# Small norm operations moved between engines, GpSimd's readout one half-step later, and the second norm two half-steps later

## The chip, the core and the metric

One NeuronCore of a Trainium2 chip runs the whole program. The metric is device time in microseconds (us); of a profiled execution the span from the first to the last instruction is known too. Engines are TensorE (PE; its weight loads are PEld), VectorE (DVE), ScalarE (ACT), GpSimd (POOL) and SyncE (SP), which only issues DMAs. Each runs its own instruction list in order and waits on semaphores for the others. A wait holds up everything behind it on that engine.

## The reference: a Mamba layer, then a mixture of experts

The input is x of shape (32, 512, 256), all in float32. Cut to what matters here:

```python
x = x + attn(layernorm(x))                 # attn(x) itself returns m + skip
x = x + ffn(layernorm(x))

# attn: norm again (with ln_g, ln_b), in_proj to xp and z, causal conv of 4 taps, silu,
# x_proj to dt, B, C; dt = softplus(dt_proj(dt)); then for each of 512 channels and 16 states
h = exp(dt * A) * h + dt * u * B           # a scan over the 512 steps
y = sum over states of h * C  + u * D
# y * silu(z), out_proj, gelu, gated linear unit, + skip

# ffn: shared expert silu(x@g) * (x@u) @ down, times sigmoid(x@gate);
# router softmax, top 8 of 64 experts, capacity 128, gather, expert MLP, weighted scatter
```

Both layer norms have no weights: (x - mean) / sqrt(var + eps). A norm of a row is computed as x * rstd + shift, with shift = -mean * rstd. The skip of the first half needs x plus its norm, which is x * (1 + rstd) + shift; 1 + rstd is called `keep`.

## The kernel before: how the work is laid out

The kernel walks over the 32 sequences. For each there is one *turn* of 32 half-steps (s = 0 to 31): the 512 channels are taken in two halves of 256, and each half has 16 states, so half-step s is one state of one half. In a half-step:

- GpSimd computes the scan's input three half-steps ahead (`scan_input`, line 381) into a ring `hs` of 8 buffers.
- ScalarE computes the decays exp(dt * A) two half-steps ahead (`decays`, line 506), into one of two PSUM pairs; it may only overwrite a pair once the state that stood there has been read.
- VectorE runs the scan (line 1173). For 16 of the half-steps (the table `ON_POOL`) the scan's result goes back into the ring and GpSimd multiplies it by C (`read_state`, line 390); for the others it stays in PSUM and VectorE multiplies it (line 1183).
- TensorE adds the products up over the states (line 810), two half-steps behind (`LAG`).

Between these, every turn does the preparation (`prep_at`) of the next sequence and the end (`post_at`) of the previous one: output projection, gelu, gated unit, the second norm, router, and the shared expert. Tables of half-steps say where each piece stands on each engine. Half-step 21, say, is a place in four lists, not a time. The router's and the shared expert's projections all go through one PSUM bank (`pobank`), so each waits until its predecessor has been read.

The parts that matter for the change, before it:

- Second norm, of the previous sequence: VectorE takes the moments at s = 15 (`moments_x1`, line 1046), ScalarE the reciprocal root at 15 (lines 519, 522), VectorE the shift at 16 (`shift_x1`, line 1066), ScalarE the normed rows at 16 (`norm_x1`, line 544), TensorE transposes them at 17 (line 897), ScalarE reads them at 17 (line 631), TensorE computes the router's logits at 18 (line 904), VectorE reads them at 20 (line 1105), and the shared expert's first projection follows at 19 on TensorE (line 919).
- First norm, of the sequence after the next: moments on VectorE at s = 21, reciprocal roots on ScalarE at 26, and at 30 VectorE computes the shifts (`shifts_x`, line 1060) and `keep` (line 1062). ScalarE uses them a turn later (lines 529, 536).

Turns 2 to 29 run in a hardware loop with two turns to an iteration; the others are written out. Behind the turns comes the part with the routed experts, which the change doesn't touch.

Of the kernel before, what the change touches and what calls it, by code (L numbers as in the profile page):

```python
# [12 lines left out]
P = 128  # L13
# [27 lines left out]
def mamba_moe(nc, x, vectors, in_wT, conv_w, x_wT, dt_wT, a_log, out_wT, glu_wT, router_w, sgu_w, sdown_w, egu_w, edown_w, out, counts, table, ends, bc):  # L41
    ctx = ExitStack()
    with ctx:
# [313 lines left out]
        def _(pool):  # L357
# [50 lines left out]

            def turn(b, h, prep, post):
                p = b + 1  # L410
                for s in range(NS):
                    if s == SIZES[1]:
                        step_sizes(b, 1)
                    if s == INPUTS[1]:
                        step_inputs(b, h, 1)
                    if prep and s == SIZES[0]:
                        step_sizes(p, 0)
                    if prep and s == INPUTS[0]:
                        step_inputs(p, 1 - h, 0)
                    to = ahead(b, h, s, LEAD, prep)  # L420
                    if to:
                        scan_input(*to)
                    if s in ON_POOL:
                        read_state(b, h, s)

            step_sizes(0, 0)
            step_inputs(0, 0, 0)
            for n in range(LEAD):
                scan_input(0, 0, 0, n)
            turns(pool, turn)  # L430

# [54 lines left out]
        def _(act):  # L486
# [22 lines left out]
            def scales_x(k):  # L509
                act.wait_ge(ln0, 3 * k + 2)  # L510
                act.activation(rstd[:, 0, :].unsqueeze(2), mv[:, 0, :, 1:2], ACT.Ln, bias=EPS)
                act.activation(rstd[:, 1, :].unsqueeze(2), mv[:, 0, :, 1:2], ACT.Ln, bias=EPS * EPS,
                               scale=1.0 + EPS).then_inc(scales0_ready, 1)
                act.wait_ge(scales0_ready, 4 * k + 1)
                act.activation(rstd[:, 0:2, :], rstd[:, 0:2, :], ACT.Exp, scale=-0.5).then_inc(scales0_ready, 1)

            def scales_x1(k):
                act.wait_ge(ln2, 3 * k + 2)
                act.activation(rstd[:, 2, :].unsqueeze(2), mv[:, 1, :, 1:2], ACT.Ln, bias=EPS)\
                    .then_inc(scales2_ready, 1)  # L520
                act.wait_ge(scales2_ready, 3 * k + 1)
                act.activation(rstd[:, 2, :], rstd[:, 2, :], ACT.Exp, scale=-0.5).then_inc(scales2_ready, 1)

            def norm_x(p):
                act.wait_ge(scales0_ready, 4 * p + 4)
# [14 lines left out]
            def norm_x1(q):  # L540
                act.wait_ge(scales2_ready, 3 * q + 3)
# [496 lines left out]
        def _(dve):  # L1038
# [14 lines left out]
            def moments_x(p):  # L1053
                dve.wait_ge(x_loaded, 16 * p + 16)
                wait(dve, scales0_ready, 4 * p)
                moments(ln0, 0, p, xin)

            def shifts_x(k):
                dve.wait_ge(scales0_ready, 4 * k + 2)
                dve.scalar_tensor_tensor(shift[:, 0:2, :], mv[:, 0, :, 0].unsqueeze(1).broadcast_to([P, 2, NT]), -1.0,  # L1060
                                         rstd[:, 0:2, :], ALU.mult, ALU.mult).then_inc(scales0_ready, 1)
                dve.tensor_scalar(keep[:, :], rstd[:, 0, :], 1.0, None, ALU.add).then_inc(scales0_ready, 1)

            def shift_x1(k):
# [73 lines left out]
            def post_at(q, h, s):  # L1138
# [8 lines left out]
                if s == SHIFT2:  # L1147
                    shift_x1(q)
# [16 lines left out]
            def turn(b, h, prep, post):  # L1165
                for s in range(NS):
# [33 lines left out]
            shifts_x(1)  # L1200
# [83 lines left out]

LAG = 2
# [18 lines left out]
SHIFT2 = 16  # L1304
# [8 lines left out]
NORM2 = 16  # L1313
# [15 lines left out]
XT_AT = (17, 17)  # L1329
R_AT = 18  # L1330
# [54 lines left out]
```

## Time and profile before

| what | value |
|---|---|
| median of 3 runs | 4608.77 us (4603.74 to 4612.37) |
| the profiled execution's own time | 4609.06 us |
| its span | 4607.3 us |
| VectorE busy | 3889.2 us (84%) |
| GpSimd busy | 4003.9 us (87%) |
| TensorE busy | 3685.3 us (80%) |
| ScalarE busy | 3164.8 us (69%) |
| granted TensorE clock, mean | 0.870 |

The turns fill the time from about 80 us to about 4170 us, the routed experts the last 350 us. Busy shares are means over both. The span and the execution's own time differ by 1.8 us, and that time is 0.3 us from the median. In the rows further on a line number such as L1066 is the line of the kernel before.

### The profile page before, as it was taken

How to read it: one execution, taken by the hardware profiler on the slowest of the kernel's cores; microseconds unless marked ns; L12 is line 12 of the kernel's file. 1: busy time of each engine (PE TensorE's matmuls, PEld its weight loads, DVE VectorE, ACT ScalarE, POOL GpSimd, SP SyncE). 2: the span in 40 equal slices, each digit the busy share in tenths (PEclk: the TensorE clock that was granted, in tenths of full speed). 3: DMA queues.
4: the chain of work that ended last, by engine and by line, in shares of the span. 5: the costliest groups of instructions: out<-in, count | busy, mean ns of one | idle time of the engine just before them, and what ended most of it. 6: DMA issues, size and time to landing. Idle time of an engine off the chain costs nothing.

```text
span 4607.3 us, 55489 instructions
## 1 busy us (share of the span) xinstructions
PE 3685.3 (80%) x16000; PEld 2374.8 (52%) x16000; DVE 3889.2 (84%) x4054; ACT 3164.8 (69%) x4931; POOL 4003.9 (87%) x1934
## 2 busy tenths in 40 slices
PE   4688888888888888888888888888888888877455
PEld 2455555555555555555555555555555555553344
DVE  4899889998989989998999899998999899993433
ACT  4677777777777777777877777777777777763111
POOL 3999889998999989998989999899999898991576
PEclk7789888899889989898989988898988898888666
DMA  3222222222222222222222212222222222210665
GB/s 121 88 99 81 70 97 83 73 99 100 95 99 97 68 86 91 66 95 99 99 95 99 90 61 99 83 70 99 99 98 97 100 66 84 91 57 17 174 158 131
DMA packets 147381, 423.29 MB, mean 92 GB/s; under 512 B 15521, under 2 KB 98657, under 8 KB 113777
## 3 DMA queue, kind: packets, MB, share of 16 engines
q1 hardware_dynamic: 123504, 362.73, 21.3%
q0 software_dynamic: 23552, 56.64, 6.5%
q8 instruction: 154, 2.52, 0.2%
q14 instruction: 171, 1.39, 0.1%
HBM read 333.17 MB, written 52.59 MB: 84 GB/s over the span
## 4 chain that ended last, share of the span: by engine, by line
DVE 27%; issue 23%; PE 19%; POOL 18%; ACT 9%; DMA 2%; DVEq 1%; POOLq 0%; ACTq 0%; SPq 0%
POOL hs L381 11%; DVE ps L1173 10%; DVE hs L1173 6%; POOL hs L390 4%; PE ps L871 4%; ACT ps L506 3%; PE ps L810 3%; PE ps L834 3%; PE ps L880 2%; PE ps L854 2%; DVE xc L1075 2%; PE ps L799 2%; ACT L488 1%; DVE stats L1046 1%; PE ps L904 1%
## 5 line engine op out<-in xcount | busy, mean ns | idle before, releaser
L381 POOL TENSOR_TENSOR hs<-dtu,b_all 128x1024 f32<-128x1024 f32 x1024 | 2426.8, 2422 | 0.8
L506 ACT ACTIVATE ps<-dt,neg_a 128x512 f32<-128x512 f32 x2048 | 1326.3, 683 | 506.4 <-DVE hs L1183 288.9
L390 POOL TENSOR_TENSOR hs<-hs,c_all 128x1024 f32<-128x1024 f32 x512 | 1228.4, 2399 | 311.5 <-DVE hs L1173 311.2
L1173 DVE TENSOR_TENSOR_SCAN hs<-ps,hs 128x1024 f32<-128x1024 f32 x512 | 1167.5, 2281 | 190.4 <-ACT ps L506 153.5
L810 PEld LDWEIGHTS ps<-ident,hs 128*128 128x128 f32 x8192 | 1042.8, 153 | 503.0 <-issue 421.7
L810 PE MATMUL ps<-ident,hs 128*128 128x128 f32 x8192 | 1170.7, 294 | 88.2 <-issue 46.7
L1173 DVE TENSOR_TENSOR_SCAN ps<-ps,hs 128x1024 f32<-128x1024 f32 x512 | 1169.5, 2284 | 64.4 <-ACT ps L506 61.6
L1183 DVE TENSOR_TENSOR hs<-ps,c_all 128x1024 f32<-128x1024 f32 x512 | 626.2, 1223 | 28.9
L919 PE MATMUL ps<-mT,w_sgu 128*128 128x512 f32 x1024 | 508.5, 620 | 86.7 <-ACT hid L660 43.1
L834 PE MATMUL ps<-xnT,w_in 128*128 128x512 f32 x512 | 273.1, 660 | 88.4 <-DVE xc L1075 86.1
L1075 DVE SCALAR_TENSOR_TENSOR xc<-ps,cw_sb,xc 128x509 f32<-128x509 f32 (+2 forms) x384 | 285.5, 743 | 34.3 <-ACT xc L559 25.2
L919 PEld LDWEIGHTS ps<-mT,w_sgu 128*128 128x128 f32 x1024 | 177.6, 193 | 247.5 <-issue 126.6
L880 PE MATMUL ps<-mT,w_glu 128*128 128x512 f32 x512 | 250.4, 611 | 58.0 <-ACT mT L618 45.4
L841 PE MATMUL ps<-w_in,xnT 128*128 128x512 f32 x512 | 286.2, 688 | 12.6 <-ACT sz L566 6.0
L927 PE MATMUL ps<-w_sd,hid 128*128 128x256 f32 x1024 | 238.0, 385 | 16.6 <-DVE mT L1134 15.7
L871 PE MATMUL ps<-hid,w_out 128*128 128x512 f32 x512 | 233.1, 598 | 1.5 <-ACT hid L608 0.9
L854 PE MATMUL ps<-xd,w_dt 32*128 32x512 f32 x256 | 205.2, 891 | 31.0 <-ACT dt L594 29.6
L927 PEld LDWEIGHTS ps<-w_sd,hid 128*128 128x128 f32 x1024 | 189.3, 190 | 52.8 <-DVE mT L1134 23.3
L834 PEld LDWEIGHTS ps<-xnT,w_in 128*128 128x128 f32 x512 | 96.6, 201 | 221.6 <-DVE xc L1075 130.5
L488 ACT ACT_TABLE_LOAD x161 | 206.6, 1283 | 3.6 <-PEq L1356 0.8
L888 PE MATMUL ps<-ident,hid 128*128 128x128 f32 x256 | 56.4, 360 | 181.5 <-DVE xn L1096 179.0
L841 PEld LDWEIGHTS ps<-w_in,xnT 128*128 128x128 f32 x512 | 109.3, 227 | 128.0 <-issue 108.2
(121 smaller groups left out, 4507.4 us busy)
## 6 DMA issues: line engine op xcount, KB each, us to landing
b_all<-bc SPq DMA_DIRECT2D x128, 1024.0 KB, 6.1
c_all<-bc SPq DMA_DIRECT2D x128, 1024.0 KB, 7.6
dt<-dtu POOLq DMA_DIRECT2D x64, 512.0 KB, 5.6
table<-rows SPq DMA_DIRECT2D x32, 640.0 KB, 3.8
xin<-x SPq DMA_DIRECT2D x32, 512.0 KB, 3.6
out<-mT SPq DMA_DIRECT2D x32, 512.0 KB, 3.8
c_all<-egu_w SPq DMA_DIRECT2D x64, 256.0 KB, 2.8
c_all<-edown_w SPq DMA_DIRECT2D x64, 128.0 KB, 2.9
```

Of the source, the lines that this page charges most:

```text
L381: pool.tensor_tensor(ring(h, hf, n), dtu[:, JH * hf:JH * hf + JH, :], b_all[:, n, :].unsqueeze(1).broadcast_to([P, JH, L]), ALU.mult)\
L390: pool.tensor_tensor(ring(h, hf, n), ring(h, hf, n), c_all[:, n, :].unsqueeze(1).broadcast_to([P, JH, L]), ALU.mult)\
L506: i = act.activation(state_of(n)[:, k, :], dt[:, j, :], ACT.Exp, scale=neg_a[:, j, n:n + 1])
L810: m = pe.matmul(ybank[:, i, k * P:(k + 1) * P], ring(h, hf, n)[:, k, i * P:(i + 1) * P], ident[:, :], start=False, stop=(n == N - 1), is_t ...
L834: m = pe.matmul(prbank, w_in[:, f, col * P:(col + 1) * P], xnT[:, f, :], start=(f == 0), stop=(f == FM - 1))
L841: m = pe.matmul(prbank, xnT[:, f, i * P:(i + 1) * P], w_in[:, f, DI:2 * DI], start=(f == 0), stop=(f == FM - 1))
L871: m = pe.matmul(pobank, w_out[:, j, f * P:(f + 1) * P], yT[:, j, :], start=(j == 0), stop=(j == J - 1))
L919: m = pe.matmul(pobank, w_sgu[:, f, block * P:(block + 1) * P], x2T[:, f, :], start=(f == 0), stop=(f == FM - 1))
L927: m = pe.matmul(po_tok[:, i, :], hid[:, k, (2 * c + i) * P:(2 * c + i + 1) * P], w_sd[:, k, :], start=(k == 0), stop=(k == KS - 1))
L1075: dve.scalar_tensor_tensor(conv_part(h, j)[:, back:L], prbank[:, 0:L - back], cw_sb[:, j, k:k + 1], conv_part(h, j)[:, back:L], ALU.mult, ...
L1173: dve.tensor_tensor_scan(inputs if s in ON_POOL else whole, whole, inputs, 0.0, ALU.mult, ALU.add).then_inc(state_ready, 1)
L1183: dve.tensor_tensor(ring(h, hf, n), state_of(n), c_all[:, n, :].unsqueeze(1).broadcast_to([P, JH, L]), ALU.mult)\
```

## The change

The small operations move, three tables shift, and a constant is new:

- `shifts_x` and `shift_x1` go from VectorE to GpSimd. [...]
- `keep` goes from VectorE to ScalarE (one instruction of 128x4, line 539).
- With `BEHIND = 1` GpSimd reads a state out one half-step later: at place s it computes input s + 3 and then reads state s - 1, not s.
- The second norm moves by two half-steps (`SHIFT2`, `NORM2` 16 to 18), its transposes by one (`XT_AT` 17 to 18), the logits by one (`R_AT` 18 to 19), and with them VectorE's reading of the logits (20 to 21). The shared expert's projections stay.

```diff
@@ GpSimd
+            def shifts_x(k):
+                pool.wait_ge(scales0_ready, 5 * k + 3)
+                pool.tensor_tensor(shift[:, 0:2, :], rstd[:, 0:2, :], mv[:, 0, :, 0].unsqueeze(1).broadcast_to([P, 2, NT]),
+                                   ALU.mult).then_inc(scales0_ready, 1)
+
+            def shift_x1(k):
+                pool.wait_ge(scales2_ready, 4 * k + 3)
+                pool.tensor_tensor(shift[:, 2, :], rstd[:, 2, :], mv[:, 1, :, 0], ALU.mult).then_inc(scales2_ready, 1)
...
+                    if post and s == SHIFT2:
+                        shift_x1(b - 1)
+                    if s == SHIFT0 and not (isinstance(b, int) and b + 2 >= B):
+                        shifts_x(b + 2)
                     to = ahead(b, h, s, LEAD, prep)
                     if to:
                         scan_input(*to)
-                    if s in ON_POOL:
-                        read_state(b, h, s)
-
+                    if s - BEHIND in ON_POOL:
+                        read_state(b, h, s - BEHIND)
+                    elif post and s < BEHIND and NS + s - BEHIND in ON_POOL:
+                        read_state(b - 1, 1 - h, NS + s - BEHIND)
+
+            shifts_x(0)
             step_sizes(0, 0)
             step_inputs(0, 0, 0)
             for n in range(LEAD):
                 scan_input(0, 0, 0, n)
+            shifts_x(1)
             turns(pool, turn)
@@ ScalarE, scales_x and scales_x1
+                act.activation(mv[:, 0, :, 0:1], mv[:, 0, :, 0:1], ACT.Identity, scale=-1.0).then_inc(scales0_ready, 1)
-                act.wait_ge(scales0_ready, 4 * k + 1)
+                act.wait_ge(scales0_ready, 5 * k + 1)
                 act.activation(rstd[:, 0:2, :], rstd[:, 0:2, :], ACT.Exp, scale=-0.5).then_inc(scales0_ready, 1)
+                act.wait_ge(scales0_ready, 5 * k + 3)
+                act.activation(keep[:, :], rstd[:, 0, :], ACT.Identity, bias=1.0).then_inc(scales0_ready, 1)
...
+                act.activation(mv[:, 1, :, 0:1], mv[:, 1, :, 0:1], ACT.Identity, scale=-1.0).then_inc(scales2_ready, 1)
@@ VectorE
-            def shifts_x(k):
-                dve.wait_ge(scales0_ready, 4 * k + 2)
-                dve.scalar_tensor_tensor(shift[:, 0:2, :], mv[:, 0, :, 0].unsqueeze(1).broadcast_to([P, 2, NT]), -1.0,
-                                         rstd[:, 0:2, :], ALU.mult, ALU.mult).then_inc(scales0_ready, 1)
-                dve.tensor_scalar(keep[:, :], rstd[:, 0, :], 1.0, None, ALU.add).then_inc(scales0_ready, 1)
-
-            def shift_x1(k):
-                dve.wait_ge(scales2_ready, 3 * k + 2)
-                dve.scalar_tensor_tensor(shift[:, 2, :], mv[:, 1, :, 0], -1.0, rstd[:, 2, :], ALU.mult, ALU.mult)\
-                    .then_inc(scales2_ready, 1)
@@ tables
+BEHIND = 1
-SHIFT2 = 16
+SHIFT2 = 18
-NORM2 = 16
+NORM2 = 18
-XT_AT = (17, 17)
-R_AT = 18
+XT_AT = (18, 18)
+R_AT = 19
```

The instruction lists show what this does to the order. On TensorE, in turn 1 (written out) from s = 17 to 19; `rows` are the normed rows to be transposed, `xd,w_dt` the projection of the next sequence's step sizes, `w_r` the router, `w_sgu` the shared expert, `ident,hs` the sum of a state. Before:

```order
L897 MATMUL ps<-ident,rows 128x128 x8
L854 MATMUL ps<-xd,w_dt 128x512
L799 MATMUL ps<-ident,xc 128x128 x8
L810 MATMUL ps<-ident,hs 128x128 x8
L904 MATMUL ps<-w_r,mT 128x65 x8
L854 MATMUL ps<-xd,w_dt 128x512
L810 MATMUL ps<-ident,hs 128x128 x8
L919 MATMUL ps<-mT,w_sgu 128x512 x2
```

The same place on TensorE in the changed kernel (line numbers are 25 higher):

```order
L879 MATMUL ps<-xd,w_dt 128x512
L824 MATMUL ps<-ident,xc 128x128 x8
L835 MATMUL ps<-ident,hs 128x128 x8
L922 MATMUL ps<-ident,rows 128x128 x8
L879 MATMUL ps<-xd,w_dt 128x512
L835 MATMUL ps<-ident,hs 128x128 x8
L929 MATMUL ps<-w_r,mT 128x65 x8
L944 MATMUL ps<-mT,w_sgu 128x512 x2
```

The transposes now stand behind the first sum of the second half, and the logits directly ahead of the shared expert's first projection, which uses the same bank.

On ScalarE, in the same turn from s = 16 to 19; `ps<-dt,neg_a` are the decays of one half-step (here of s = 18 to 21), `rows` the second norm, `mT<-ps` the transposes' reading, `xs` the kept sum, `dtu` and `dt` the step sizes. Before:

```order
L506 ACTIVATE ps<-dt,neg_a 128x512 x2
L544 ACTIVATE rows<-xn,shift,rstd 128x256 x4
L587 COPY xd<-ps 64x512
L506 ACTIVATE ps<-dt,neg_a 128x512 x2
L631 COPY mT<-ps 128x512 x2
L593 ACTIVATE dtu<-ps,vecs 128x512
L594 ACTIVATE dt<-ps,vecs 128x512
L506 ACTIVATE ps<-dt,neg_a 128x512 x2
L536 ACTIVATE xs<-xin,shift,keep 128x256 x4
L593 ACTIVATE dtu<-ps,vecs 128x512
L594 ACTIVATE dt<-ps,vecs 128x512
L506 ACTIVATE ps<-dt,neg_a 128x512 x2
```

The same place on ScalarE in the changed kernel:

```order
L527 ACTIVATE ps<-dt,neg_a 128x512 x2
L612 COPY xd<-ps 64x512
L527 ACTIVATE ps<-dt,neg_a 128x512 x2
L618 ACTIVATE dtu<-ps,vecs 128x512
L619 ACTIVATE dt<-ps,vecs 128x512
L527 ACTIVATE ps<-dt,neg_a 128x512 x2
L569 ACTIVATE rows<-xn,shift,rstd 128x256 x4
L656 COPY mT<-ps 128x512 x2
L561 ACTIVATE xs<-xin,shift,keep 128x256 x4
L618 ACTIVATE dtu<-ps,vecs 128x512
L619 ACTIVATE dt<-ps,vecs 128x512
L527 ACTIVATE ps<-dt,neg_a 128x512 x2
```

The norm and the transposes' reading now stand between the decays of s = 20 and those of s = 21, together with the kept sum and the second step size.

On GpSimd, in the same turn from s = 13 to 23; `dtu,b_all` are scan inputs, `hs,c_all` read states. Before:

```order
L381 TENSOR_TENSOR hs<-dtu,b_all 128x1024
L390 TENSOR_TENSOR hs<-hs,c_all 128x1024
L381 TENSOR_TENSOR hs<-dtu,b_all 128x1024 x4
L390 TENSOR_TENSOR hs<-hs,c_all 128x1024
L381 TENSOR_TENSOR hs<-dtu,b_all 128x1024 x2
L390 TENSOR_TENSOR hs<-hs,c_all 128x1024
```

The same place on GpSimd in the changed kernel, from the reading of state 14:

```order
L390 TENSOR_TENSOR hs<-hs,c_all 128x1024
L381 TENSOR_TENSOR hs<-dtu,b_all 128x1024
L390 TENSOR_TENSOR hs<-hs,c_all 128x1024
L381 TENSOR_TENSOR hs<-dtu,b_all 128x1024
L416 TENSOR_TENSOR shift<-rstd,mv 128x4
L381 TENSOR_TENSOR hs<-dtu,b_all 128x1024 x3
L390 TENSOR_TENSOR hs<-hs,c_all 128x1024
L381 TENSOR_TENSOR hs<-dtu,b_all 128x1024 x2
L390 TENSOR_TENSOR hs<-hs,c_all 128x1024
```

Ahead of the reading of state 19 there are five inputs since state 15 was read, not four (19 to 22 before, 20 to 23 and the shift now).

## Rows read from the trace of the kernel before

**Rows 1.** Two turns: length; busy PE, PEld, DVE, ACT, POOL; clock, DMA share, GB/s.
```profile
2129.22:2256.18 126.96, 107.03 (x472) 68.68 (x472) 116.49 (x110) 96.56 (x150) 114.21 (x53) 0.90 0.25 86
2256.18:2385.53 129.35, 107.68 (x480) 68.65 (x480) 118.36 (x112) 98.18 (x153) 121.60 (x57) 0.90 0.27 93
```

**Rows 2.** Waits, 1000 to 4000 us: total us, times, longest.
```profile
POOL hs L390 <- DVE hs L1173: 241.5, 100, 4.3
...
DVE hs L1173 <- ACT ps L506: 116.1, 81, 3.6
...
DVE hs L1173 <- POOL hs L381: 7.2, 2, 3.6
```

**Rows 3.** Groups by line, whole span: busy us, mean ns | idle before.
```profile
L1066 DVE SCALAR_TENSOR_TENSOR shift<-mv,rstd 128x4 f32<-128x4 f32 x32 | 55.6, 1737 | 0.5 <-ACT rstd L522 0.5
...
L1062 DVE TENSOR_SCALAR keep<-rstd 128x4 f32<-128x4 f32 x32 | 36.2, 1132 | 0.0
...
L1060 DVE SCALAR_TENSOR_TENSOR shift<-mv,rstd 128x8 f32<-128x8 f32 x32 | 27.2, 849 | 15.9 <-ACT rstd L515 15.9
...
L522 ACT ACTIVATE rstd<-rstd 128x4 f32<-128x4 f32 x32 | 6.6, 206 | 1.0
L407 POOL MEMSET dt<- 128x2 f32 x64 | 6.5, 101 | 9.1 <-POOL dtu L405 8.7
```

**Rows 4.** VectorE's timeline, s = 16 to 27: start, duration, [idle before].
```profile
2198.23 1.79 DVE L1066 SCALAR_TENSOR_TENSOR shift<-mv,rstd 128x4 f32<-128x4 f32 x1
...
2206.72 1.21 DVE L1183 TENSOR_TENSOR hs<-ps,c_all 128x1024 f32<-128x1024 f32 x1
...
2213.49 0.42 DVE L1105 COPY lg<-ps 128x260 f32<-128x260 f32 x1
...
2215.92 2.29 DVE L1173 TENSOR_TENSOR_SCAN hs<-ps,hs 128x1024 f32<-128x1024 f32 x1 [1.56 <-ACT ps L506]
...
2237.28 2.28 DVE L1173 TENSOR_TENSOR_SCAN hs<-ps,hs 128x1024 f32<-128x1024 f32 x1
```

**Rows 5.** VectorE, shift and scan 21 of the first and last of eleven turns.
```profile
266.44 1.80 DVE L1066 SCALAR_TENSOR_TENSOR shift<-mv,rstd 128x4 f32<-128x4 f32 x1
...
284.15 2.29 DVE L1173 TENSOR_TENSOR_SCAN hs<-ps,hs 128x1024 f32<-128x1024 f32 x1 [1.56 <-ACT ps L506]
...
3611.69 1.81 DVE L1066 SCALAR_TENSOR_TENSOR shift<-mv,rstd 128x4 f32<-128x4 f32 x1
...
3632.56 2.29 DVE L1173 TENSOR_TENSOR_SCAN hs<-ps,hs 128x1024 f32<-128x1024 f32 x1 [3.61 <-ACT ps L506]
```

**Rows 6.** ScalarE's timeline in the turn of rows 4, s = 16 to 25.
```profile
2200.05 2.08 ACT L544 ACTIVATE rows<-xn,shift,rstd 128x256 f32<-128x256 f32 x4 [0.41 <-DVE shift L1066]
...
2206.08 0.59 ACT L631 COPY mT<-ps 128x512 f32<-128x512 f32 x1 [0.74 <-PE ps L897]
...
2209.70 2.06 ACT L536 ACTIVATE xs<-xin,shift,keep 128x256 f32<-128x256 f32 x4
...
2214.02 0.68 ACT L594 ACTIVATE dt<-ps,vecs 128x512 f32<-128x512 f32 x1
2214.59 1.30 ACT L506 ACTIVATE ps<-dt,neg_a 128x512 f32<-128x512 f32 x2
...
2235.52 2.58 ACT L506 ACTIVATE ps<-dt,neg_a 128x512 f32<-128x512 f32 x4
```

**Rows 7.** TensorE's timeline in the same turn, s = 17 to 20.
```profile
2205.39 0.66 PE L897 MATMUL ps<-ident,rows 128*128 128x128 f32 x4 [1.62 <-ACT mT L631]
...
2214.26 1.88 PE L919 MATMUL ps<-mT,w_sgu 128*128 128x512 f32 x4
2215.97 1.04 PE L810 MATMUL ps<-ident,hs 128*128 128x128 f32 x8
2218.62 1.98 PE L919 MATMUL ps<-mT,w_sgu 128*128 128x512 f32 x4 [1.61 <-ACT hid L660]
```

**Rows 8.** The 3 us behind the wait in rows 7; columns as in rows 1.
```profile
2206.00:2209.00 3.00, 3.00 (x12) 2.06 (x12) 3.00 (x3) 2.27 (x4) 0.94 (x1) 0.63 0.03 5
```

More of the change, by code:

```diff
@@ L429, in _ @@
                 scan_input(0, 0, 0, n)
+            shifts_x(1)
             turns(pool, turn)
+            for s in range(NS - BEHIND, NS):
+                if s in ON_POOL:
+                    read_state(B - 1, 1, s)
+            shift_x1(B - 1)
             pool.wait_ge(prep_full, B * PREP_USES)
@@ L520, in scales_x1 @@
                     .then_inc(scales2_ready, 1)
-                act.wait_ge(scales2_ready, 3 * k + 1)
+                act.activation(mv[:, 1, :, 0:1], mv[:, 1, :, 0:1], ACT.Identity, scale=-1.0).then_inc(scales2_ready, 1)
+                act.wait_ge(scales2_ready, 4 * k + 1)
                 act.activation(rstd[:, 2, :], rstd[:, 2, :], ACT.Exp, scale=-0.5).then_inc(scales2_ready, 1)
             def norm_x(p):
-                act.wait_ge(scales0_ready, 4 * p + 4)
+                act.wait_ge(scales0_ready, 5 * p + 5)
                 wait(act, prep_full, (p - 1) * PREP_USES + PREP_T[1] + 1)
@@ L540, in norm_x1 @@
             def norm_x1(q):
-                act.wait_ge(scales2_ready, 3 * q + 3)
+                act.wait_ge(scales2_ready, 4 * q + 4)
                 wait(act, rows_stored, 16 * q)
@@ L1054, in moments_x @@
                 dve.wait_ge(x_loaded, 16 * p + 16)
-                wait(dve, scales0_ready, 4 * p)
+                wait(dve, scales0_ready, 5 * p)
                 moments(ln0, 0, p, xin)
-            def shifts_x(k):
-                dve.wait_ge(scales0_ready, 4 * k + 2)
-                dve.scalar_tensor_tensor(shift[:, 0:2, :], mv[:, 0, :, 0].unsqueeze(1).broadcast_to([P, 2, NT]), -1.0,
-                                         rstd[:, 0:2, :], ALU.mult, ALU.mult).then_inc(scales0_ready, 1)
-                dve.tensor_scalar(keep[:, :], rstd[:, 0, :], 1.0, None, ALU.add).then_inc(scales0_ready, 1)
-            def shift_x1(k):
-                dve.wait_ge(scales2_ready, 3 * k + 2)
-                dve.scalar_tensor_tensor(shift[:, 2, :], mv[:, 1, :, 0], -1.0, rstd[:, 2, :], ALU.mult, ALU.mult)\
-                    .then_inc(scales2_ready, 1)
             def conv(p, h, j):
@@ L1146, in post_at @@
                     moments_x1(q)
-                if s == SHIFT2:
-                    shift_x1(q)
                 if s == R_AT + AFTER_R:
@@ L1191, in turn @@
                         moments_x(b + 2)
-                    if s == SHIFT0 and not (isinstance(b, int) and b + 2 >= B):
-                        shifts_x(b + 2)
             moments_x(0)
-            shifts_x(0)
             for s in range(NS):
@@ L1199, in _ @@
             moments_x(1)
-            shifts_x(1)
             turns(dve, turn)
```

## The prediction

> **What bounds the kernel now.** I first read the two windows that cover one loop iteration [rows 1]. The reader is to see that no engine is full: of 127.0 and 129.4 us VectorE works 116.5 and 118.4, GpSimd 114.2 and 121.6. A turn is thus as long as a ring of waits makes it, and moving work off VectorE is worth only what that ring gives back. Second came the waits [rows 2]. GpSimd stands still for VectorE's scans, 241.5 us in 3000, while VectorE waits for GpSimd's inputs twice, 7.2 us in all. VectorE waits for ScalarE's decays: 116.1 us ahead of the scans that write the ring. So the ring is VectorE and ScalarE, with TensorE where ScalarE waits for it. Third, the timeline from s = 16 on [rows 4, 6, 7], because the norm's chain lies there. I call scan 21 the scan of s = 21.
>
> **What leaves VectorE.** Per sequence: L1066 1.74 us, L1062 1.13, L1060 0.85 [rows 3]. They compute on 4 to 8 elements; what they mostly do is stand. Together 3.7 us a turn, 119 us in all, and no row shows VectorE idle just ahead of them in the loop, so each pushes what is behind it. What each is worth depends on the next wait.
>
> *At s = 30 and 31.* Behind L1060 and L1062 comes scan 31, whose decays are long ready (the wait is ahead of scan 30). With 0.15 us of overlap between instructions the gain is 0.85 + 1.13 - 0.15 = 1.8 us a turn. I take it whole; zero is the other end.
>
> *At s = 16.* Scan 17 moves up by 1.79 - 0.08 = 1.7 us, and with it state 18's readout, which ended at 2206.72 + 1.21 = 2207.93 [rows 4]: now 2206.2, 8.0 us behind the place L where L1066 began (2198.23). Scan 21 started at L + 17.7 in this turn. But this turn was a good one: over eleven turns the distance is 17.7 to 20.9, mean 19.0; the first and the last of them stand in [rows 5].
>
> **What the second norm's new place costs.** Now everything stands between ScalarE's decays of 20 and of 21. The decays of 20 must wait for state 18's readout, at L + 8.0. From there ScalarE's list is unbroken, in durations of rows 6 and 7 less the 0.1 us by which successors overlap: decays of 20, half of 2.58 less overlap, 1.25; the norm 2.08; transposes and their readings, which alternate over one bank, twice (0.66 + 0.59) with hand-overs, 2.55; kept sum 1.95; reading of the second step size 1.15; decays of 21, 1.30. Sum 10.3, so scan 21 starts at L + 18.3. Before, the kept sum lay in the shadow of TensorE (ScalarE idled behind it), and the norm ahead of two waits; now they add. Against the mean of 19.0 this is 0.7 us earlier; against the turn of rows 4 it is 0.6 later.
>
> TensorE's clock: after a wait of 1.62 us ahead of a transpose [rows 7] the granted clock of the following 3 us was 0.63 [rows 8], between full (1.00, 2.4 GHz) and half (0.50, 1.2 GHz). In the new order TensorE has done the sum of state 16 about 2.5 us before the norm ends, so I expect the same fall there. Two transposes at half clock cost up to 2 x 0.45 us; I take 0.5 on the mean. So scan 21 comes 0.2 us earlier than now, bounds 1.3 earlier and 1.0 later.
>
> **What the late logits cost.** The shared expert's first projection may not start until VectorE has read the logits, since the bank is the same. Before, that reading was at s = 20 (2213.49) and the projection at 2214.26, that is 1.66 us ahead of scan 21; the second one started 2.70 behind the start of scan 21 [rows 4, 7]. Now the reading stands behind scan 21: 2.20 for the scan, 0.42 for the reading, 0.05 hand-over: the first projection starts at 2.67, lasts 1.82 to its successor, the sum of a state takes 0.88, and the second projection starts at 5.37. It is 2.7 us later against scan 21. From there to scan 27 the work is in series: four projections and three of z through two banks, a reading by ScalarE behind each, then the silu, whose end lets the decays of 27 start. Those ended at 2235.52 + 1.30 = 2236.8, and scan 27 started at 2237.28 [rows 4, 6]: 0.5 us of slack. So 2.7 - 0.5 = 2.2 us a turn arrive at scan 27. Bounds: 0, if the projections can catch up in the waits of the series, and 2.7.
>
> **ScalarE's additions.** Three tiny instructions a turn, each like L522's 0.21 us [rows 3], or 0.1 where they overlap. At s = 15 they lie ahead of a wait. At s = 26 two of them and a wait for the Exp's end stand ahead of the decays of 29: before, 0.5 us of idle covered that, but these decays now follow the late silu, so I count 0.3 us a turn (0 to 0.5).
>
> **GpSimd.** Two tiny products a turn. The nearest rows are the memset of L407, 0.10 us, and L1066's mean of 1.74 if GpSimd were held as VectorE was; I take 0.2, nearer the memset, as the operands are as small. Either is covered: GpSimd idles 10 us a turn (241.5 / 3000 x 128). [...] Readout one half-step later: VectorE's waits for inputs are the most it can remove, 7.2 us in 3000, so nearly nothing in the loop. In turn 0, which has no end-of-sequence work, GpSimd does limit, and one readout less ahead of the inputs is worth about 2 us, once. The price: each sum on TensorE may find its state read 2.4 us later; GpSimd's use of its idle time ahead of states 19 and 21 makes up for that, so 0, bounds -0.3 and +2.4 a turn.
>
> **The sum.** Per turn: -0.2 (scan 21) + 2.2 (scan 27) + 0.3 (s = 26) - 1.8 (s = 30) = +0.5 us. Over the 30 turns that have both preparation and end, +15 us; start -2. The profiled execution took 4609.06 us (0.3 above the median of the runs shown), so 4609 + 13 = **4622 us**.
>
> **Rivals.**
>
> *A, faster.* The late logits are hidden. For it: the second projection waited 1.61 us for ScalarE [rows 7], which shows that ScalarE, not TensorE, set the pace there, so a later first projection may cost less than it is late. Against: my count of the second projection's start already leaves that wait out, and behind it the readings and projections follow each other on one bank. Then -0.2 + 0.3 - 1.8 = -1.7 a turn, 30 turns, start: 4556 us.
>
> *B, no change.* Of the 2.2 us about 0.5 are made up, so the terms cancel: 4600 to 4618 us. For it: the terms are near each other; one tenth of a microsecond a turn is 3 us in all.
>
> *C, much slower.* TensorE has nothing to do between the logits and their reading by VectorE, 3 to 4 us. If its clock falls there, the first projections take twice 1.9 us; with the first at half clock and the second partly, +2.3 us a turn, 4622 + 70 = 4692 us. For it: a fall after 1.62 us of wait [rows 7, 8]. Against: the fall that I already count at the transposes makes the logits take longer and fills this wait. The Trainium skill (TensorE: Matmul & The Clock Gate, section "HAM oscillation — how this bites in real kernels") describes a clock that falls again at every wait of this kind in a loop; the trace agrees that a wait is followed by a fall, not that each is.
>
> *D, slower by GpSimd.* The later readout holds up the sums of states 28 and 29, just ahead of the turn's end: up to +2.4 a turn, 4690 us. It decides where GpSimd is not ahead of where it is now. Against: its 10 us of idle time.
>
> **Chances.** Forecast 0.40, A 0.27, B 0.18, C 0.10, D 0.05. A measurement of this kernel can tell about 0.2%, 9 us, from no change. Faster: A and a little of the forecast, 0.29; within: B and the forecast's lower edge, 0.21; slower 0.50. The range reaches from a little below A to a little below C: 4550 to 4680 us; the forecast's own is 4605 to 4645.
>
> **What would show it.** Scan 21 at about 18 us behind the end of state 16's readout with an idle time ahead of it of 4 to 5 us (1.6 to 3.6 now), for ScalarE; ScalarE's decays of 20, norm, readings, kept sum, step size, decays of 21 without a wait but TensorE's. TensorE's first w_sgu projection waiting for VectorE's reading of the logits, 3 to 4 us. Scan 27 at 23.5 us behind scan 21 (21.4 now) with a wait for ScalarE. No gap between the end-of-sequence addition at s = 30 and scan 31. GpSimd's tiny products under 0.3 us. I am wrong if VectorE's idle time a turn falls, if the projections' waits shrink again before scan 27, or if GpSimd's busy share passes 95%.

## The result, and the profile after

The changed kernel took 4692.81 us (median of 4 runs, 4689.94 to 4696.01), the kernel before, on the same chip, 4610.57 (4603.74 to 4625.88): a ratio of 1.0174, 95% interval 1.0147 to 1.0200. It is 1.7% slower, 82 us. I had predicted 4622 us, in a range of 4550 to 4680: the sign is right, the loss is six times as large and outside the range. The profiled execution of the changed kernel took 4696.01 us, with a span of 4693.8 (before 4607.3).

The windows of one iteration of the loop, columns as in [rows 1]. The first turn of an iteration has an even number (here 16), the second an odd one (17), and the way from an odd turn to the next even one leads over the loop's back edge:

```profile
2171.69:2302.07 130.38, 113.75 (x472) 73.02 (x472) 114.14 (x108) 95.08 (x149) 114.41 (x56) 0.83 0.23 80
2302.07:2434.46 132.39, 106.93 (x481) 69.14 (x480) 113.84 (x109) 99.53 (x158) 122.21 (x58) 0.91 0.28 94
```

VectorE is 2.4 and 4.5 us less busy than in [rows 1], which is the work that left it, and the turns are 3.4 and 3.0 us longer. TensorE works 6.7 us more in the first of the two, at a mean clock of 0.83 where it was 0.90. The waits from 1000 to 4000 us, as [rows 2]:

```profile
DVE hs L1185 <- ACT ps L527: 213.1, 98, 5.7
POOL hs L381 <- PE ps L835: 166.2, 69, 3.7
...
POOL hs L390 <- DVE hs L1185: 125.8, 80, 2.4
ACT hid L685 <- PE ps L944: 124.1, 69, 4.5
...
DVE hs L1185 <- issue: 46.8, 22, 4.4
```

VectorE waits 97 us longer for ScalarE's decays, ScalarE waits for TensorE's shared-expert projections (L685 <- L944), and 22 scans wait for nothing that the profile shows ("issue"; 6 before). 11 of the 22, with 44 of the 46.8 us, are a scan 0 behind the back edge. GpSimd's inputs wait for TensorE's sums, which no row of before had in that size; that looks like the culprit and is not (run e3). GpSimd's two tiny products took 211 and 203 ns, as priced:

```profile
L411 POOL TENSOR_TENSOR shift<-rstd,mv 128x8 f32<-128x8 f32 x32 | 6.8, 211 | 9.4 <-ACT rstd L537 9.4
...
L416 POOL TENSOR_TENSOR shift<-rstd,mv 128x4 f32<-128x4 f32 x32 | 6.5, 203 | 47.9 <-ACT rstd L547 47.9
```

To find the place I took the start of every scan out of VectorE's timeline, and compared the distances between some of them. Means over turns 4 to 28, in us, before | after:

```
stretch          even turns       odd turns        sum of both   on record, two turns
scan 0 to 16     64.24 | 63.14    63.11 | 63.94      -0.3          0
scan 16 to 21    21.77 | 22.69    22.64 | 22.31      +0.6         -0.4
scan 21 to 27    21.36 | 26.26    21.55 | 23.59      +6.9         +4.4
scan 27 to 30     9.49 |  9.50     9.49 |  9.50       0.0         +0.6
scan 30 to 0     10.79 |  8.95    12.96 | 13.06      -1.7         -3.6
a turn          127.66 | 130.55  129.76 | 132.40     +5.5         +1.0
```

15 times 5.5 is 83 us, the whole of the difference. Two rows carry most of the miss: scan 21 to 27 in even turns, where 4.9 us are lost and not 2.2, and scan 30 to 0 in odd turns, where nothing is won. A third, smaller piece is scan 16 to 21, 1.0 us a pair of turns.

TensorE's timeline (start, duration, [idle before]) behind the logits (L929) of turn 16, whose scan 21 starts at 2257.17, then of turn 17, whose scan 21 starts at 2388.39:

```profile
2255.90 3.52 PE L929 MATMUL ps<-w_r,mT 128*128 128x65 f32 x16
2259.93 3.78 PE L944 MATMUL ps<-mT,w_sgu 128*128 128x512 f32 x4 [0.52 <-DVE lg L1119]
2263.51 1.91 PE L835 MATMUL ps<-ident,hs 128*128 128x128 f32 x8
2265.22 2.28 PE L944 MATMUL ps<-mT,w_sgu 128*128 128x512 f32 x4
...
2387.12 2.75 PE L929 MATMUL ps<-w_r,mT 128*128 128x65 f32 x16
2391.05 1.98 PE L944 MATMUL ps<-mT,w_sgu 128*128 128x512 f32 x4 [1.18 <-DVE lg L1119]
2392.88 1.04 PE L835 MATMUL ps<-ident,hs 128*128 128x128 f32 x8
2393.75 1.95 PE L944 MATMUL ps<-mT,w_sgu 128*128 128x512 f32 x4
```

In the odd turn the first projection starts 2.66 us behind scan 21 and the second 5.36, where the prediction had 2.67 and 5.37. In the even turn the first takes 3.78, the sum behind it 1.91, and the second starts 8.05 behind. Windows of the same kernel: the 20 us around that place in turn 16, then the 6 us ahead of scan 21 in turn 17 and the 11 behind it.

```profile
2246.00:2266.00 20.00, 17.37 (x56) 11.93 (x55) 12.99 (x16) 12.62 (x22) 9.86 (x5) 0.50 0.46 184
...
2382.50:2388.60 6.10, 6.10 (x22) 4.26 (x21) 0.88 (x2) 5.14 (x10) 3.14 (x2) 0.50 0.19 47
2389.00:2400.00 11.00, 9.82 (x41) 5.64 (x41) 10.78 (x15) 6.56 (x11) 9.12 (x6) 1.00 0.73 299
```

The granted clock is half (1.2 GHz) in both stretches ahead of the logits' reading. In the odd turn it is full again (2.4 GHz) when the projection starts; in the even turn it stays at half through the projection and the sum.

### The profile page after: what moved, and what is told of

Same layout as the page of the kernel before. It is cut to its first block, busy times and chain, and to the rows that moved or that the text cites. A ratio compares the mean times of both kernels' runs of the same rounds, so it can differ in the third digit from the quotient of the medians.

```text
span 4693.8 us, 55595 instructions
## 1 busy us (share of the span) xinstructions
PE 3748.6 (80%) x16000; PEld 2423.9 (52%) x16000; DVE 3786.5 (81%) x3958; ACT 3160.4 (67%) x5027; POOL 4017.7 (86%) x1998
## 3 DMA queue, kind: packets, MB, share of 16 engines
q1 hardware_dynamic: 123504, 362.73, 21.7%
## 4 chain that ended last, share of the span: by engine, by line
POOL 32%; issue 25%; PE 18%; DVE 14%; ACT 8%; DMA 2%; POOLq 0%; DVEq 0%; ACTq 0%; SPq 0%
POOL hs L381 18%; POOL hs L390 8%; DVE ps L1185 6%; PE ps L944 4%; DVE hs L1185 4%; PE ps L835 4%; ACT ps L527 2%; POOL dtu L405 2%; PE ps L952 2%; PE ps L866 2%; ACT L509 1%; PE ps L824 1%; ACT rows L569 1%; PE ps L922 1%; POOL hs L459 1%
## 5 line engine op out<-in xcount | busy, mean ns | idle before, releaser
L390 POOL TENSOR_TENSOR hs<-hs,c_all 128x1024 f32<-128x1024 f32 x512 | 1214.5, 2372 | 161.1 <-DVE hs L1185 160.9
L835 PEld LDWEIGHTS ps<-ident,hs 128*128 128x128 f32 x8192 | 1060.0, 154 | 523.6 <-issue 461.4
L835 PE MATMUL ps<-ident,hs 128*128 128x128 f32 x8192 | 1187.5, 297 | 92.2 <-issue 52.8
L944 PE MATMUL ps<-mT,w_sgu 128*128 128x512 f32 x1024 | 540.2, 653 | 58.0 <-DVE hid L1142 29.8
L944 PEld LDWEIGHTS ps<-mT,w_sgu 128*128 128x128 f32 x1024 | 188.2, 205 | 223.9 <-issue 137.3
L952 PE MATMUL ps<-w_sd,hid 128*128 128x256 f32 x1024 | 238.2, 386 | 26.4 <-DVE mT L1148 25.5
L685 ACT COPY hid<-ps 128x512 f32<-128x512 f32 x128 | 74.9, 585 | 187.2 <-PE ps L944 187.2
```

The lines of the kernel that those rows point to most:

```text
L390: pool.tensor_tensor(ring(h, hf, n), ring(h, hf, n), c_all[:, n, :].unsqueeze(1).broadcast_to([P, JH, L]), ALU.mult)\
L835: m = pe.matmul(ybank[:, i, k * P:(k + 1) * P], ring(h, hf, n)[:, k, i * P:(i + 1) * P], ident[:, :], start=False, stop=(n == N - 1), is_t ...
L944: m = pe.matmul(pobank, w_sgu[:, f, block * P:(block + 1) * P], x2T[:, f, :], start=(f == 0), stop=(f == FM - 1))
L952: m = pe.matmul(po_tok[:, i, :], hid[:, k, (2 * c + i) * P:(2 * c + i + 1) * P], w_sd[:, k, :], start=(k == 0), stop=(k == KS - 1))
```

## The experiments

Times are medians; the kernel before took 4604 to 4610 us beside them. "T" is the theory that the result suggested: the late logits cost 2.2 us a turn and more where the projection meets half clock, the back edge takes a fixed time, and the place of GpSimd's readout costs nothing. Each run's text gives T as it stood before that run. Code is shortened.

**e1, e2: where the chain stands.** The tables alone on the kernel before, and the tables taken back from the changed kernel:

```
e1, before.py                        e2, after.py
-SHIFT2 = 16      +SHIFT2 = 18       -SHIFT2 = 18      +SHIFT2 = 16
-NORM2 = 16       +NORM2 = 18        -NORM2 = 18       +NORM2 = 16
-XT_AT = (17, 17) +XT_AT = (18, 18)  -XT_AT = (18, 18) +XT_AT = (17, 17)
-R_AT = 18        +R_AT = 19         -R_AT = 19        +R_AT = 18
```

> The kernel before, with only the second norm's chain later: shift and norm at s = 18, transposes at 18, logits at 19, read at 21. Shifts and kept sum stay on VectorE, GpSimd reads out where it did. Theory T (the late chain costs: the first projection behind scan 21's reading of the logits 2.2 us a turn, and TensorE at half clock in it in every second turn, 3.0 us): scan 21 to scan 27 in 26.4 us in even and 23.4 in odd turns, as in the changed kernel; and as VectorE's product of 1.8 us now stands at s = 18 just ahead of the norm, scan 21 another 0.5 later. 30 x (2.2 + 1.5 + 0.5) = +126: 4735 us, 4690 to 4760. Rival G (GpSimd's later readout is what costs): no later readout here, so no change but VectorE's: 4600 to 4625 us, and scan 21 to scan 27 stays at 21.4.

Measured: 4724.05 us, ratio 1.0249 (1.0216 to 1.0282), 114 us slower. Scan 21 to 27 is 23.4 to 26.5 us, mean 25.1 in turns of either kind. T's size holds; its even and odd turns do not. Which turns keep the low clock differs from kernel to kernel (in e4 too, 25.3 and 25.1), only the mixture is much the same (25.1 here, 24.9 in the changed kernel).

> The changed kernel with the chain put back: shift and norm at s = 16, transposes 17, logits 18, read at 20. The small operations stay off VectorE, GpSimd's readout stays one half-step later. Theory T: scan 21 to scan 27 back at 21.4 us in every turn (+0 against the kernel before), 1.7 us a turn won at s = 16 if GpSimd gives the shift in time, 1.8 at s = 30 in even turns only, since the loop's back edge takes it in the odd ones: 4611 - 30 x 1.7 x (half of it kept at scan 21) - 15 x 1.8 = about 4558 us, 4530 to 4600. Rival G: the later readout still holds up TensorE's sums, so 4680 us or more.

Measured: 4485.25 us, ratio 0.9741 (0.9705 to 0.9777): 125 us faster than before, 208 faster than the changed kernel. Scan 21 to 27 is 21.7 and 21.6 us. The later chain is the whole loss, and what is left of the change is a large gain, outside T's range (4530 to 4600): scan 16 to 21 takes 20.3 and 18.5 us, against 21.8 and 22.6 before.

The two parts do not simply add. The later chain costs 114 us on the kernel before (e1) and 208 on the kernel with the small operations moved; those win 125 us with the chain in its old place and only 31 with the late one (4724 to 4693). The place is scan 16 to 21: 22.5 us with the late chain, whether the small operations have moved or not (e1 and the changed kernel), and 22.2 and 19.4 with the old one (before and e2).

**e3, e8: GpSimd's readout in its own half-step**, in the changed kernel and in e2.

```
-BEHIND = 1
+BEHIND = 0
```

> The changed kernel with GpSimd reading a state out in its own half-step again, all else as changed. Theory T: the readout's place costs nothing, 4680 to 4705 us, and scan 21 to scan 27 stays 26.4 and 23.4 us. Rival G: what GpSimd's input waits for TensorE's sums (218 us in the changed kernel, 0.8 before) is the loss, so it goes and the time falls to 4610 to 4630 us.

Measured: 4691.94 us, the same as the changed kernel; scan 21 to 27 is 25.9 and 24.1 us, not 26.4 and 23.4. GpSimd's two groups, of the changed kernel and then of e3 (busy, mean ns | idle before):

```profile
L381 POOL TENSOR_TENSOR hs<-dtu,b_all 128x1024 f32<-128x1024 f32 x1024 | 2427.7, 2401 | 218.5 <-PE ps L835 217.6
...
L390 POOL TENSOR_TENSOR hs<-hs,c_all 128x1024 f32<-128x1024 f32 x512 | 1214.5, 2372 | 161.1 <-DVE hs L1185 160.9
```
```profile
L381 POOL TENSOR_TENSOR hs<-dtu,b_all 128x1024 f32<-128x1024 f32 x1024 | 2426.6, 2416 | 0.8
L390 POOL TENSOR_TENSOR hs<-hs,c_all 128x1024 f32<-128x1024 f32 x512 | 1218.6, 2380 | 374.5 <-DVE hs L1185 373.4
```

218 us of waiting for TensorE are gone and come back as waiting for VectorE. GpSimd waits the same time elsewhere, and the kernel's time stays. The most striking new wait of the profile costs nothing.

> The changed kernel with the chain put back to s = 16 to 20 and GpSimd's readout in its own half-step, so that of the change only the small operations off VectorE are left. Theory T: the readout's place is worth nothing here too, 4475 to 4495 us. Rival: in a faster turn GpSimd, at 90% of its time, does count, and the later readout is what let it pass: 4500 to 4530 us.

Measured: 4484.53 us, e2's time, at a busy share of GpSimd of 90%. The readout's place is worth nothing there either.

**e4: four turns in an iteration** of the loop, in the changed kernel; e7 the same edit on e2.

```
-with eng.Fori(1, B // 2 - 1) as it:
-    turn(it * 2, 0, True, True)
-    turn(it * 2 + 1, 1, True, True)
+with eng.Fori(0, B // 4 - 1) as it:
+    turn(it * 4 + 2, 0, True, True)
+    turn(it * 4 + 3, 1, True, True)
+    turn(it * 4 + 4, 0, True, True)
+    turn(it * 4 + 5, 1, True, True)
```

> The changed kernel with four turns in an iteration of the loop in place of two: 7 iterations, so 7 back edges fewer of 14. Theory T (VectorE's way from scan 30 over the loop's back edge to scan 0 takes 13.0 us whatever stands in it, against 8.95 where the next turn follows in line): 7 x 4.05 = -28 us, 4665 us. Rival: the wait at the edge is for other engines' work, which only moves to the next wait: 4685 to 4700 us.

Measured: 4668.29 us, 24.5 less than the changed kernel, close to T's 28. The 14 iterations had 13 back edges (the last one leaves the loop), the 7 have 6: 3.5 us an edge.

> The changed kernel with the chain put back to s = 16 to 20, and four turns in an iteration of the loop. If the back edge costs 4.0 us whatever the turn's length (theory T): 4485 - 28 = 4457 us. If the two gains lie on one another: 4470 to 4485.

Measured: 4463.49 us, 22 less than e2: 3.1 us an edge, between the two expectations. The turn behind an edge gives some of the 4 us back; that ScalarE catches up in VectorE's wait is my guess and was not tried.

**e6: the first norm's shifts and the kept sum alone**, on the kernel before.

```
-dve.scalar_tensor_tensor(shift[:, 0:2, :], mv..., -1.0, rstd[:, 0:2, :], mult, mult)
-dve.tensor_scalar(keep[:, :], rstd[:, 0, :], 1.0, None, ALU.add)
+act.activation(mv[:, 0, :, 0:1], mv[:, 0, :, 0:1], ACT.Identity, scale=-1.0)
+act.activation(keep[:, :], rstd[:, 0, :], ACT.Identity, bias=1.0)
+pool.tensor_tensor(shift[:, 0:2, :], rstd[:, 0:2, :], mv..., ALU.mult)
```

> The kernel before, with only the first norm's shifts and the kept sum off VectorE (L1060 and L1062, at s = 30); the second norm's shift stays, all tables as before, GpSimd's readout in place. Prediction on record: 1.8 us a turn. Theory T: scan 30 to scan 0 in 8.95 us in even turns (10.8 before), and still 13.0 in odd turns, since the loop's back edge sets that: 14 x 1.8 = 25 us, 4585 us. Rival: the prediction's 1.8 in every turn, 4557 us, and 11.2 us from scan 30 to scan 0 in odd turns.

Measured: 4580.80 us, ratio 0.9936 (0.9916 to 0.9956). Scan 30 to scan 0 is 8.9 to 9.0 us in every even turn and 12.9 to 13.1 over every back edge, as T has it; the prediction's 1.8 in every turn falls. From e6 to e8 only the second norm's shift (L1066) leaves VectorE, and ScalarE negates its mean: another 96 us, 3.2 a turn.

**e5, e9: TensorE kept busy**, in the changed kernel. e9 has e5's edit and the last two lines:

```
+def keep_busy(count):
+    for i in range(count):
+        pe.transpose(pobank[:, i % 4 * P:(i % 4 + 1) * P], ident[:, :], ident[:, :])
 start_y:  +keep_busy(8) ahead of its waits, for the second half
 turn_x2:  +keep_busy(12) ahead of the wait for the norm
 logits:   -for i in range(NT):
           +for i in (0, 1, 2, 3, 0, 1, 2, 3, 0, 1):
```

> The changed kernel, and TensorE does idle transposes of the identity matrix into the bank that is free there: 8 ahead of its wait for the gated output at s = 18 and 12 ahead of its wait for the second norm, so that it hardly stands still before the transposes. Nothing is taken off any wait. Theory T (in every second turn the clock is at half from that wait until past the first projection, which so costs 3.0 us): scan 21 to scan 27 in 23.4 us in all turns, and up to 0.9 us less from scan 16 to scan 21 as the transposes take 0.6 in place of 1.1: 4693 - 15 x 3.0 - 30 x (0 to 0.9) = 4620 to 4650 us. Rival: the series behind scan 21 is late for another reason (the sum of state 18, which stands between the projections and waits for GpSimd's readout), and the clock only follows: 4690 us or more.

Measured: 4687.06 us, between T's range and the rival's. The expectation is missed: scan 16 to 21 is 0.7 shorter, but scan 21 to 27 is 25.4 and 25.7 us on the mean of even and odd turns, in none under 25.0, not 23.4. TensorE's timeline of e5 (scan 21 starts at 2259.67):

```profile
2254.05 0.65 PE L930 MATMUL ps<-ident,rows 128*128 128x128 f32 x4 [0.68 <-ACT mT L656]
...
2256.62 1.90 PE L937 MATMUL ps<-w_r,mT 128*128 128x65 f32 x16
2262.34 3.78 PE L952 MATMUL ps<-mT,w_sgu 128*128 128x512 f32 x4 [3.82 <-DVE lg L1127]
```

The transposes and the logits now run at full clock and end 1.15 us ahead of scan 21. But the reading still stands behind scan 21, so TensorE waits 3.82 us for it, and the projection is at half clock again, now in every turn. This is the clock fall of the prediction's rival C: one measured at the projection, in a wait of 3 to 4 us. The low clock at the projection thus has two causes that replace each other: carried through from an earlier fall, or a new fall in the longer wait.

> The kernel with the idle transposes, and the logits computed two and a half times in place (the same matmuls again, the same values), so that TensorE ends them about 1.7 us behind the start of scan 21 in place of 1.15 ahead of it: its wait for VectorE's reading falls from 3.8 us to about 1. The reading itself is no later, since it stands behind scan 21. Theory T, amended (the clock falls in TensorE's wait between the logits and their reading where it is long, or stays at half from an earlier wait where it is short): the first projection at full clock, 2.0 us, scan 21 to scan 27 in 23.4 us in all turns; 30 x 2.1 = 63 us less than the 4687 with the idle transposes alone: 4624 us, and 4630 allowing for some turns that fall. Rival (the clock is not what the projections wait for): 4685 us or more, and 25.5 us from scan 21 to scan 27.

Measured: 4657.74 us, 29 less than e5 and not 63. Odd turns, then even turns, in TensorE's timeline:

```profile
2364.82 4.58 PE L937 MATMUL ps<-w_r,mT 128*128 128x65 f32 x40
2370.54 1.98 PE L952 MATMUL ps<-mT,w_sgu 128*128 128x512 f32 x4 [1.14 <-DVE lg L1127]
```
```profile
2232.91 8.63 PE L937 MATMUL ps<-w_r,mT 128*128 128x65 f32 x40
2242.07 3.54 PE L952 MATMUL ps<-mT,w_sgu 128*128 128x512 f32 x4 [0.52 <-DVE lg L1127]
```

In all 14 odd turns the wait is short, the projection takes 1.98, and scan 21 to 27 is 23.4 us (25.7 in e5). In even turns it is 23.4 to 29.1 us: in the one shown the clock had fallen ahead of the logits, the repeated logits then took 8.6 us, and scan 21 to 27 took 29.1 us, 3.7 more than the mean of e5's even turns. In the odd turns the first projection starts 2.66 us behind scan 21, as in e5: so they show that the clock, and nothing else, is the 2.3 us. The even turns show that filling can backfire.

**e10, e11: no loop**, the 28 turns one behind the other, on e2 and on the kernel before.

```
-with eng.Fori(1, B // 2 - 1) as it: ...
+for b in range(2, B - 2):
+    turn(b, b % 2, True, True)
```

> The changed kernel with the chain put back to s = 16 to 20, and the 28 turns of the loop written one behind the other, no loop. If the back edge costs 4.0 us each, 14 of them (theory T): 4485 - 57 = 4428 us, or 4441 if each saves what four turns in an iteration saved (22 us for 7 edges, 3.1 each). If a program without a loop must fetch its instructions as dearly as the edge does: 4480 us or more.

Measured: 4439.82 us, ratio 0.9633 (0.9600 to 0.9667): 45 less than e2, 3.5 us for each of the 13 edges (the expectation counts 14). Scan 30 to 0 is 8.9 to 9.0 in every turn. The 3.5 is a net figure: without the loop scan 21 to 27 is 21.0 us in every turn (21.7 in e2), scan 16 to 21 is 20.4 (19.4), and why is open.

> The kernel before with the 28 turns of the loop written one behind the other. Theory T (the edge costs in the kernel before too: 12.95 us from scan 30 to scan 0 over it, 10.8 on the mean in line): 14 x 2.1 = -30 us, so 4576, and a little more back where the wait at the edge let ScalarE catch up: 4575 to 4595 us. Rival (before, the edge cost nothing, as VectorE's small operations stood in its place): 4600 to 4610 us.

Measured: 4570.00 us, ratio 0.9913 (0.9887 to 0.9939), 38 us or 2.9 an edge: the edge cost in the kernel before as well, and the gain is a little above the expected range. Here too scan 21 to 27 fell, from 21.4 and 21.6 to 21.0 us, which is some 12 of the 38.

**e12: e10 with TensorE filled in one short wait.**

```
 turn_x2:
+if f == 1 and q + 2 < B:
+    use_prep(q + 2, PREP_D[0])
+    for i in range(6):
+        pe.transpose(prbank[:, i % 4 * P:(i % 4 + 1) * P], ident[:, :], ident[:, :])
```

> The kernel with the chain put back and no loop, and TensorE does six idle transposes of the identity into the preparation's bank in its wait of 0.93 us between the two groups of the norm's transposes. Theory T (that wait is what lets the clock fall; start of the sum and the sum behind it then take 1.1 and 1.04 us in place of 1.8 and 1.9, and scan 21 waits 2.0 us for what follows from them): scan 21 up to 1.6 us earlier, 30 x 1.6 = -48, 4392 us. Rival (the clock falls all the same at another short wait, or the second group of transposes is held up by the filling): 4430 to 4450 us.

Measured: 4407.11 us, ratio 0.9553 (0.9516 to 0.9590): the fastest version, 4.5% under the kernel before. TensorE's timeline of e10, then of e12, behind the first group of the norm's transposes (L921, L925): L823 and L834 are the start of the sum and a sum.

```profile
2244.24 0.66 PE L921 MATMUL ps<-ident,rows 128*128 128x128 f32 x4 [0.93 <-ACT mT L655]
2244.82 1.12 PE L878 MATMUL ps<-xd,w_dt 32*128 32x512 f32 x2
2245.88 1.77 PE L823 MATMUL ps<-ident,xc 128*128 128x128 f32 x8
2247.44 1.91 PE L834 MATMUL ps<-ident,hs 128*128 128x128 f32 x8
```
```profile
2225.51 0.66 PE L925 MATMUL ps<-ident,rows 128*128 128x128 f32 x4 [0.27 <-ACT mT L655]
2226.10 1.12 PE L878 MATMUL ps<-xd,w_dt 32*128 32x512 f32 x2
2227.15 1.09 PE L823 MATMUL ps<-ident,xc 128*128 128x128 f32 x8
2228.08 1.04 PE L834 MATMUL ps<-ident,hs 128*128 128x128 f32 x8
```

Where 0.66 of the wait are filled, the clock stays, start and sum take 1.6 us less, and scan 16 to 21 takes 18.8 us (20.4 in e10), as expected; 0.4 a turn is lost again, so 33 us are won and not 48. Half of the 0.4 lies between scan 21 and 27: in every third turn the shared expert's first projection takes 3.67 us, at half clock, where it takes 1.98 in the others.

## Why the prediction was half right

The steps account for the miss, a pair of turns: scan 21 to 27 +2.5 us, the back edge +1.9, scan 16 to 21 +1.0, ScalarE's additions -0.6, scan 0 to 16 -0.3; together 4.5 us, 15 times that is 68 of the 71 us between 4622 and 4693. That rivals C (4692) and D (4690) name the measured time is luck: C's price was 2.3 us in every turn, and the clock cost 2.7 in even turns alone; D's cause is ruled out by e3.

*Late logits, +2.2 at scan 27: right in mechanism and size, where the clock is full.* Odd turns have scan 21 to 27 in 23.4 us (predicted 23.5) and every step between at its place.

*TensorE's clock behind the logits: this step failed.* The price of a half-clock projection (+2.3, rival C) was worked out, and given a chance of 0.10 because "the fall that I already count at the transposes makes the logits take longer and fills this wait". It does fill it: the wait is 0.5 to 1.2 us and not 3 to 4. But filling with half-clock work did not bring the clock back in even turns, and where I made the logits quick (e5), the wait came back and took the clock. Cost: 4.9 in place of 2.2 us in even turns, less 0.2 that the odd ones saved, 2.5 us a pair of turns beyond the record.

The sum took the fall at the transposes as their own cost, 0.5 us, and let it end there. The trace of before showed that it need not. In turn 27, the second one of [rows 5], the clock fell behind a wait of 1.81 us and stayed at half for 13.5 us of unbroken work, up to and into the first projection, which took 2.80 us and not 1.88; turns 3, 9 and 29 have the same.

```profile
3618.87 0.66 PE L897 MATMUL ps<-ident,rows 128*128 128x128 f32 x4 [1.81 <-ACT mT L631]
...
3624.51 3.52 PE L904 MATMUL ps<-w_r,mT 128*128 128x65 f32 x16
...
3631.72 2.80 PE L919 MATMUL ps<-mT,w_sgu 128*128 128x512 f32 x4
```
```profile
3620.00:3633.50 13.50, 13.50 (x47) 9.80 (x46) 8.93 (x8) 8.03 (x15) 7.38 (x4) 0.50 0.49 190
```

In the changed kernel the low stretch of turn 16 lasts from 2245.7 to 2266.1: it begins 3.6 us ahead of the transposes (2249.31), earlier than the wait of 1.43 us just ahead of them, where I had expected the fall, and ends past the projection. In turn 17 it lasts from 2382.1 to 2388.9 and ends ahead of the projection. The Trainium skill (TensorE: Matmul & The Clock Gate, section "HAM oscillation — how this bites in real kernels") has the clock fall anew in every round of a loop that waits long in each round. With waits of 3.8 us the trace agrees, in all turns of e5; with waits about 1 us it fell in some turns of the same program and not in others, as in e9.

*s = 30, -1.8 a turn: right in even turns, nothing in odd ones.* "I take it whole" was the mistake. Three boundaries between turns: the last shared-down projection of TensorE, VectorE's addition behind it and the next scan 0: before where L1062 was held up (turn 15), before where it wasn't (turn 7), and after (turn 15).

```profile
2120.72 3.72 PE L927 MATMUL ps<-w_sd,hid 128*128 128x256 f32 x16 [0.64 <-DVE mT L1134]
...
2126.97 0.86 DVE L1134 SCALAR_TENSOR_TENSOR mT<-ps,small,xn 128x256 f32<-128x256 f32 x2
...
2129.22 2.29 DVE L1173 TENSOR_TENSOR_SCAN hs<-ps,hs 128x1024 f32<-128x1024 f32 x1 [1.39 <-ACT ps L506]
```
```profile
1093.08 3.72 PE L927 MATMUL ps<-w_sd,hid 128*128 128x256 f32 x16 [0.63 <-DVE mT L1134]
...
1097.09 0.87 DVE L1134 SCALAR_TENSOR_TENSOR mT<-ps,small,xn 128x256 f32<-128x256 f32 x2
...
1101.64 2.29 DVE L1173 TENSOR_TENSOR_SCAN hs<-ps,hs 128x1024 f32<-128x1024 f32 x1 [3.69 <-issue]
```
```profile
2162.91 3.72 PE L952 MATMUL ps<-w_sd,hid 128*128 128x256 f32 x16 [0.82 <-DVE mT L1148]
...
2171.69 2.29 DVE L1185 TENSOR_TENSOR_SCAN hs<-ps,hs 128x1024 f32<-128x1024 f32 x1 [4.15 <-issue]
```

Scan 0 starts 4.78, 4.84 and 5.06 us behind the projection's end, in all 26 edges of the two traces 4.8 to 5.3, though the addition starts anywhere from 2.3 to 5.2 ahead of scan 0. The projection's end releases VectorE's last wait of the iteration; the way over the edge seems to begin there, and what VectorE still computes lies beside it. That this is the anchor is read from the distances and was not tried by itself; that the edge costs is shown by e4, e6, e7, e10 and e11. What the edge's time consists of is open; it is not VectorE's alone, since TensorE's first sum behind it stands 3.8 us for nothing that the profile shows (2172.13, L835). A row of the waits of before (1000 to 4000 us) should have warned me. I had not asked where these six lie: each is a scan 0 behind the edge.

```profile
DVE hs L1173 <- issue: 22.4, 6, 3.9
```

*Scan 21: forecast -0.2, measured +0.3 a turn.* The chain is the forecast one, without a wait but TensorE's: in turn 16 scan 21 starts 19.3 us behind the place that the prediction calls L (on record 18.8 with the 0.5 for the clock). The transposes cost more: both ran at half clock in that turn (1.11 and 1.12, where 0.60 to 0.66 is full), and 3.6 us lie between norm and kept sum where I had 3.05. Idle time ahead of scan 21: 5.6 and 5.2 us on the mean of even and odd turns, forecast 4 to 5.

*ScalarE's additions at s = 26, +0.3: wrong, 0.* Scan 27 to 30 is 9.5 us before and after.

*GpSimd: right on every point* (products of 0.2 us, later readout 0, e3 and e8). Its 0.2 us was a guess between two rows, 0.10 and 1.74.

*What the small operations are worth: too small.* I priced the gain at s = 16 as 1.7 us and set it off against the chain. By itself (e6 to e8) it is 3.2 us a turn. TensorE's clock moves with it: the start of the sum behind the transposes takes 1.97 us, half clock, in turns 10 to 21 of e6, and 1.09 in most odd turns of e8, where scan 16 to 21 is 18.5 us (20.2 on the mean of even ones). Against its old chain the change is a gain of 125 us, and moving the chain then loses 208.

## What to carry to other kernels

A step that is moved is priced with the clock of the engine behind it: ask in which wait TensorE will stand before the moved step and after, and price its next matmuls at both levels. A gain ahead of a loop's back edge may be hidden by the edge's own time: compare the distance over the edge with the same distance in line. The biggest new wait in a profile may be free; undo its cause before believing it.

## What the runs showed of the hardware

**The loop's back edge costs 4 us on VectorE** (13.0 against 8.95 us from scan 30 to scan 0), 2.9 to 3.5 us each in the time (e4, e7, e10, e11). The Trainium skill (Advanced Engine Details and Errata, section "Control Flow Timing") gives a compare-and-branch about 108 ns. By that page an estimate for 13 edges is 1.4 us, and e10 measured 45.

**Three of VectorE's tiny operations stood until GpSimd's running instruction ended.** They are L1060, L1062 and L1066. GpSimd's timeline before, then VectorE's:

```profile
2118.88 2.38 POOL L381 TENSOR_TENSOR hs<-dtu,b_all 128x1024 f32<-128x1024 f32 x1
2121.20 2.37 POOL L390 TENSOR_TENSOR hs<-hs,c_all 128x1024 f32<-128x1024 f32 x1
```
```profile
2120.58 0.70 DVE L1060 SCALAR_TENSOR_TENSOR shift<-mv,rstd 128x8 f32<-128x8 f32 x1
2121.21 2.39 DVE L1062 TENSOR_SCALAR keep<-rstd 128x4 f32<-128x4 f32 x1
```

L1060 ends at 2121.28, GpSimd's instruction at 2121.26; L1062 then meets the next one and ends at 2123.60 with it (2123.57). In 14 of its 32 instances it was held so, 2.4 us; in the other 18 it took 0.16. That is why its mean of 1.13 [rows 3] was a mixture, and why the prediction's 1.8 is about 0.7 or about 3 in a given turn. Not every tiny operation is held: the router's reciprocals of 128x4, from SBUF to SBUF, took 0.15 to 0.18 us, 31 of 32 inside a running GpSimd instruction. The Trainium skill (SBUF — State Buffer, section "SBUF: two separate sides") describes such a lock, held for the whole instruction, for a VectorE operation with two SBUF inputs or in a two-port mode. The trace agrees for the two products, L1060 and L1066; L1062 has one input, and no row shows its mode.
